# A graph-attention kernel in which TensorE, not VectorE, adds the gathered rows of the second pair of groups

## The chip, the cores and the metric
The kernel runs on one core of a Trainium2 chip. The metric is the device time of one execution in microseconds (us); the median of three runs counts. Engines are named TensorE (PE, its weight loads PEld), VectorE (DVE), ScalarE (ACT), GpSimd (POOL) and SP, which only issues transfers.

## What is computed
Three layers follow one another on 2500 nodes of 256 values: a GATv2 attention over 80000 edges, a lambda layer over all nodes, and a mixture of eight experts. The change touches the attention. Cut to that:

```python
xl = (x @ W_l).reshape(N, HEADS, HEAD_DIM)      # 4 heads of 64
xr = (x @ W_r).reshape(N, HEADS, HEAD_DIM)
e = xl[src] + xr[dst]
e = jnp.where(e >= 0, e, 0.2 * e)
score = jnp.einsum('ehd,hd->eh', e, att)
m = segment_max(score, dst)
ex = jnp.exp(score - m[dst])
agg = segment_sum(ex / segment_sum(ex, dst)[dst] * xl[src], dst)
```

The edges are sorted by destination. The slope is split: 0.8 times the rectified part, made in the loop below, and a linear part that comes in four extra columns of the gathered rows.

## The kernel before
A first stage (`survey`) makes xl and xr and stores them in DRAM; `attend` runs the edges; `node_update` and `experts` follow. The edges are cut into 704 groups of 128, and four groups are a step ("quad"), so there are 176 steps. Eight steps are a run (22 of them), sixteen a turn; the first and last turn are written out, the nine between are a hardware loop. `over_quads` (L928) calls each engine's `quad(q)` in order of steps, and what stands in `quad` is that engine's order of work. Engines meet only by semaphores that count steps.

For step q:
- **GpSimd** (L1069) gathers four times 128 rows of xl, of 260 values, by indirect DMA (L1084) into slot q mod 16 of a ring. It waits for ScalarE's products of step q-14 or so.
- **SP** (L1008) loads the relative destinations and 128 rows of xr (three bf16 parts), once TensorE is through with step q-4.
- **VectorE** makes the selection matrices of step q+2 (`select`, L1150; it waits until TensorE's edge matmuls of step q are done, since it overwrites their buffer), sums, rectifies, scores (L1175), builds the matrices for the sums of step q-10 (`spread`, L1183) and adds step q-12's sums to the running ones (L1197).
- **TensorE** (`edges`, L1394) makes xr[dst] as selection times xr, three bf16 matmuls for each group (L1404). In groups 0 and 1 it also adds xl[src] in PSUM by an fp32 matmul with the identity (L1409). Groups 2 and 3 come first and get no such matmul: VectorE adds their gathered rows (`sum_edges`, L1158) into SBUF. Then come the four matmuls of the sums of step q-12 (L1458).
- **ScalarE** (L1504) makes exponentials and the products with the gathered rows of step q-11 (L1513), sixteen instructions.

The edge sums of a step lie in two PSUM banks, groups 0 and 1 in one, 2 and 3 in the other; steps alternate between two such pairs of banks. The rectified products are L1164 (groups 0 and 1, from PSUM) and L1168 (groups 2 and 3, from the SBUF sum).

When a run is complete, the next eight steps close it: VectorE adds the linear part (L1213) and scans over the scores in step 0, takes the ends (L1230), carries them and makes the drop (L1255) in step 1, raises the tops (L1262, L1268) and takes them off the scores (L1274) in step 2. TensorE turns the scores (L1420, step 1), the ends (L1426, step 1, behind the sums), the carried columns (L1433, step 2) and the tops (L1438, step 3). ScalarE's decay (L1502) waits for the drop, at the front of its step 2, and its products of a new run for L1274.

## Time and profile before
| | us |
|---|---|
| runs | 1641.7, 1633.38, 1640.45; median 1640.45 |
| the profiled execution | 1640.74 |
| its span, first to last instruction | 1639.0 |
| TensorE busy | 1227.7 (75%) |
| VectorE busy | 1081.0 (66%) |
| ScalarE busy | 849.5 (52%) |
| GpSimd busy | 815.9 (50%) |
[...]

Times come from one execution taken by the hardware profiler. "Idle" is the time in which an engine ran nothing ahead of an instruction, and the releaser is what the profile takes for the end of it: "issue" if it shows none, "remote" if the event came from no engine of the list. Matmuls are pipelined, so successive ones overlap in the records, and the step from one start to the next is what they cost in the queue. An fp32 matmul appears as two records.

### The profile page before, as it was taken

The numbers are of one execution on the slowest core, as the hardware profiler recorded it, in microseconds if no ns is written. First come the engines' busy times: TensorE is split into PE (matmuls) and PEld (weight loads), VectorE is DVE, ScalarE is ACT, GpSimd is POOL, SyncE is SP. The second block draws the span as 40 slices with busy tenths as digits, with TensorE's granted clock in tenths as the row PEclk, the third lists the DMA queues.
The fourth block names the chain that finished last, engine by engine and source line by source line (L and its number), as shares of the span: only waits on it lengthen the run. The fifth ranks groups of instructions, "written<-read, shape, count | busy, mean of one in ns | idle before, by whom it ended". The sixth has DMA issues, their size and how long they took to land. (4 is left out here: it accounts for less than half of the span.)

```text
span 1639.0 us, 24939 instructions
## 1 busy us (share of the span) xinstructions
PE 1227.7 (75%) x5659; PEld 873.8 (53%) x5659; DVE 1081.0 (66%) x2307; ACT 849.5 (52%) x3252; POOL 815.9 (50%) x849
## 2 busy tenths in 40 slices
PE   7948677777778777877777876877787656399995
PEld 5426455555555555655555654655565545255663
DVE  8645767676767776777767875777577759304444
ACT  3411466765676566666666755666666713132221
POOL 5344255555565556555565555545656264402223
PEclk9978897888888989898998988888888977599998
DMA  7454356665666656666656665556755125335340
GB/s 183 139 174 121 97 155 162 159 167 149 159 154 166 160 151 159 164 166 163 163 160 165 170 161 152 154 144 169 218 145 138 40 62 174 136 104 148 103 122 17
DMA packets 167497, 237.47 MB, mean 145 GB/s; under 512 B 40112, under 2 KB 134017, under 8 KB 167406
## 3 DMA queue, kind: packets, MB, share of 16 engines
q1 hardware_dynamic: 123310, 130.22, 28.0%
q0 software_dynamic: 41216, 103.67, 24.8%
q10 hardware_dynamic: 2880, 2.66, 0.5%
q14 instruction: 71, 0.58, 0.1%
q8 instruction: 20, 0.33, 0.1%
HBM read 189.57 MB, written 48.91 MB: 146 GB/s over the span
## 5 line engine op out<-in xcount | busy, mean ns | idle before, releaser
L1084 POOL DMA_INDIRECT gathered_rows<-d_xl,e_idx x576 | 547.5, 950 | 430.3 <-ACT e_prod L1513 180.5
L1513 ACT ACTIVATE e_prod<-gathered_rows,e_prod 128x64 f32<-128x64 f32 x2728 | 678.3, 334 | 44.2 <-issue 36.8
L1458 PE MATMUL bank<-e_prod,e_selt 128*128 128x260 f32 x1408 | 407.5, 436 | 141.8 <-DMA gathered_rows<-in_src_dram,n_row_of 73.2
L1458 PEld LDWEIGHTS bank<-e_prod,e_selt 128*128 128x128 f32 x1408 | 289.9, 214 | 235.9 <-DMA gathered_rows<-in_src_dram,n_row_of 86.1
L1404 PE MATMUL bank<-e_xr,e_sel 128*128 128x256 bf16 x2112 | 334.9, 298 | 42.5 <-issue 28.6
L1158 DVE TENSOR_TENSOR e_edge<-bank,gathered_rows 128x512 f32<-128x512 f32 x176 | 119.9, 681 | 292.4 <-remote 269.3
L1404 PEld LDWEIGHTS bank<-e_xr,e_sel 128*128 128x128 bf16 x2112 | 222.3, 107 | 141.1 <-issue 67.7
L1409 PE MATMUL bank<-gathered_rows,ident 128*128 128x256 f32 x704 | 237.6, 418 | 37.8 <-issue 31.2
L1175 DVE TENSOR_REDUCE e_score<-e_edge 128x16 f32<-128x1024 f32 x176 | 213.3, 1212 | 0.3
L1084 POOL DMA_INDIRECT gathered_rows<-d_xl,src_cols x112 | 106.1, 948 | 107.5 <-issue 31.7
L1509 ACT ACTIVATE e_prod<-e_diff 128x16 f32<-128x16 f32 x176 | 39.5, 224 | 207.7 <-remote 136.9
L1409 PEld LDWEIGHTS bank<-gathered_rows,ident 128*128 128x128 f32 x704 | 119.9, 211 | 49.9 <-issue 36.1
L1183 DVE TENSOR_TENSOR e_selt<-bank,cyclic_cols 128x512 f32<-128x512 f32 x176 | 120.0, 682 | 13.8 <-remote 11.2
L1953 POOL DMA_INDIRECT out_dram<-f_out,f_index x32 | 44.8, 1399 | 159.7 <-DVE f_out L2068 154.9
L1164 DVE SCALAR_TENSOR_TENSOR e_edge<-bank,att_relu 128x512 f32<-128x512 f32 x176 | 119.7, 680 | 0.0
L1168 DVE SCALAR_TENSOR_TENSOR e_edge<-e_edge,bank 128x512 f32<-128x512 f32 x176 | 118.8, 675 | 0.0
L1975 PE MATMUL bank<-f_rowst,w_rows 128*128 128x391 f32 x256 | 87.4, 499 | 0.7 <-ACT f_rowst L2016 0.7
L1987 PE MATMUL bank<-f_hid,w_rows 128*128 128x391 f32 x256 | 85.8, 492 | 0.0
L1502 ACT ACTIVATE e_rr<-e_drop 1x4 f32<-1x4 f32 x22 | 4.5, 204 | 156.1 <-DVE e_drop L1255 133.3
L1197 DVE SCALAR_TENSOR_TENSOR e_acc<-e_acc,keep_cols,bank 128x260 f32<-128x260 f32 x154 | 73.6, 478 | 13.4 <-PE bank L1458 10.5
L1975 PEld LDWEIGHTS bank<-f_rowst,w_rows 128*128 128x128 f32 x256 | 49.2, 193 | 37.4 <-issue 2.5
L1987 PEld LDWEIGHTS bank<-f_hid,w_rows 128*128 128x128 f32 x256 | 47.9, 189 | 33.6
(315 smaller groups left out, 1102.2 us busy)
## 6 DMA issues: line engine op xcount, KB each, us to landing
e_xr<-d_xr SPq DMA_DIRECT2D x176, 192.0 KB
d_hist<-e_acc SPq DMA_DIRECT2D x176, 130.0 KB
e_drow<-d_rel SPq DMA_DIRECT2D x176, 128.0 KB
w_rows<-in_L_ffn_w_dram SPq DMA_DIRECT2D x16, 1024.0 KB, 7.2
gathered_rows<-d_xl,e_idx POOLq DMA_INDIRECT x576
d_in<-lambda_w SPq DMA_DIRECT2D x18, 350.7 KB
e_rows<-d_rows SPq DMA_DIRECT2D x22, 192.5 KB
x_rows<-in_x_dram SPq DMA_DIRECT2D x8, 512.0 KB, 4.8
```

Of the source, the lines that this page charges most:

```text
L1084: pool.indirect_dma_start(xl[:, q.slot * G + g, :], None, m.d_xl, bass.IndirectOffsetOnAxis(ap=column, axis=0)).then_inc(gathered[q.slot], 16)
L1158: dve.tensor_tensor(edge[:, b, 2:4, :], ps_edge[b][1][:, :].rearrange("p (g c) -> p g c", g=2), xl[:, q.slot * G + 2:q.slot * G + 4, 0:DIM ...
L1164: dve.scalar_tensor_tensor(out=edge[:, b, 0:2, :], in0=ps_edge[b][0][:, :].rearrange("p (g c) -> p g c", g=2), scalar=0.0, in1=m.att_relu[ ...
L1168: dve.scalar_tensor_tensor(out=edge[:, b, 2:4, :], in0=edge[:, b, 2:4, :], scalar=0.0, in1=att_relu.unsqueeze(1).to_broadcast([P, 2, DIM]) ...
L1175: dve.tensor_reduce(score[:, p, :, q.at * G:q.at * G + G].rearrange("p h g -> p g h"), edge[:, b, :, :].rearrange("p g (h c) -> p g h c", ...
L1183: dve.tensor_tensor(selt[:, b, :, :], lane_up.unsqueeze(1).to_broadcast([P, G, P]), m.cyclic[:, bass.ds(q.k * G, G)].unsqueeze(2).to_broad ...
L1404: last = pe.matmul(out, sel[:, b, g * P:g * P + P], xr[:, r, part * DIM:part * DIM + DIM], start=(part == 0), stop=(part == 2 and g >= 2))
L1409: last = pe.matmul(out, m.ident[:, :], xl[:, q.slot * G + g, 0:DIM], start=False, stop=True)
L1458: last = pe.matmul(ps_agg[b], selt[:, b, g, :], flat(prod[:, b, g, :, :]), start=(g == 0), stop=(g == G - 1))
L1513: last = act.activation(prod[:, b, g, h, 0:HEAD], xl[:, q.slot * G + g, h * HEAD:h * HEAD + HEAD], ACT.Copy, scale=prod[:, b, g, h, HEAD:H ...
L1975: last = pe.matmul(m.bank[2 + f % 2][:, 0:CAP], w1[:, q, half, f * P:f * P + P], rowst[:, q, half, :], start=(half == 0), stop=(half == 1))
L1987: last = pe.matmul(m.bank[4 + to][:, 0:CAP], w2[:, q, f, to * P:to * P + P], hid[:, f, :], start=(f == 0), stop=(f == FCH - 1))
```

## The change
TensorE adds the gathered rows in all four groups, which now go in the order 0, 1, 2, 3. `sum_edges` and its semaphore go. L1168's successor reads the sum from PSUM and the factor from SBUF, so the copy of the factor in PSUM goes too. A new semaphore `half` rises when groups 0 and 1 are done, and the first rectified product waits for it; the second waits for all four. TensorE waits for the second product of step q-2 ahead of group 2.

```diff
-            dve.tensor_copy(att_relu, m.att_relu[:, :]).then_inc(s["fixed"], 1)
...
-            def sum_edges(q):
-                b = q.slot % 2
-                dve.wait_ge(s["edges"], q.k + 1)
-                dve.wait_ge(gathered[q.slot], (q.turn + 1) * 64)
-                if q.since(2):
-                    dve.wait_ge(s["score"], q.k - 1)
-                dve.tensor_tensor(edge[:, b, 2:4, :], ps_edge[b][1][:, :].rearrange("p (g c) -> p g c", g=2),
-                                  xl[:, q.slot * G + 2:q.slot * G + 4, 0:DIM], ALU.add).then_inc(s["summed"], 1)
...
             def relus(q):
 
                 b = q.slot % 2
+                if q.since(2):
+                    dve.wait_ge(s["score"], q.k - 1)
+                dve.wait_ge(s["half"], q.k + 1)
                 dve.scalar_tensor_tensor(out=edge[:, b, 0:2, :], in0=ps_edge[b][0][:, :].rearrange("p (g c) -> p g c", g=2), scalar=0.0,
...
-                dve.wait_ge(s["summed"], q.k + 1)
-                dve.scalar_tensor_tensor(out=edge[:, b, 2:4, :], in0=edge[:, b, 2:4, :], scalar=0.0,
-                                         in1=att_relu.unsqueeze(1).to_broadcast([P, 2, DIM]),
+                dve.wait_ge(s["edges"], q.k + 1)
+                dve.scalar_tensor_tensor(out=edge[:, b, 2:4, :], in0=ps_edge[b][1][:, :].rearrange("p (g c) -> p g c", g=2), scalar=0.0,
+                                         in1=m.att_relu[:, :].unsqueeze(1).to_broadcast([P, 2, DIM]),
...
-                if live:
-                    sum_edges(q)
...
                 if q.since(2):
-                    pe.wait_ge(s["summed"], q.k - 1)
                     pe.wait_ge(s["relu"], 2 * q.k - 3)
-                for g in (2, 3, 0, 1):
+                for g in range(G):
+                    if g == 2 and q.since(2):
+                        pe.wait_ge(s["relu"], 2 * q.k - 2)
                     out = ps_edge[b][g // 2][:, g % 2 * DIM:g % 2 * DIM + DIM]
                     for part in range(3):
                         last = pe.matmul(out, sel[:, b, g * P:g * P + P], xr[:, r, part * DIM:part * DIM + DIM],
-                                         start=(part == 0), stop=(part == 2 and g >= 2))
-                    if g < 2:
-                        if g == 0:
-                            pe.wait_ge(gathered[q.slot], (q.turn + 1) * 64)
-                        last = pe.matmul(out, m.ident[:, :], xl[:, q.slot * G + g, 0:DIM], start=False, stop=True)
+                                         start=(part == 0), stop=False)
+                    if g == 0:
+                        pe.wait_ge(gathered[q.slot], (q.turn + 1) * 64)
+                    last = pe.matmul(out, m.ident[:, :], xl[:, q.slot * G + g, 0:DIM], start=False, stop=True)
+                    if g == 1:
+                        last.then_inc(s["half"], 1)
                 last.then_inc(s["edges"], 1)
...
-                act.wait_ge(s["summed"], q.k - 1)
+                act.wait_ge(s["edges"], q.k - 1)
```

## Rows read from the trace of the kernel before
**Rows 1.** The page's first part: busy time of each engine over the span.
```profile
span 1639.0 us, 24939 instructions
...
PE 1227.7 (75%) x5659; PEld 873.8 (53%) x5659; DVE 1081.0 (66%) x2307; ACT 849.5 (52%) x3252; POOL 815.9 (50%) x849
```

**Rows 2.** Windows, steady loop: us, busy (count) per engine, PEclk, DMA share, GB/s.
```profile
400.00:1100.00 700.00, 523.73 (x2619) 387.05 (x2618) 494.86 (x949) 444.32 (x1830) 397.53 (x419) 0.88 0.60 159
```

**Rows 3.** Groups by line, 400 to 1100 us: count | busy us, mean ns | idle before.
```profile
L1513 ACT ACTIVATE e_prod<-gathered_rows,e_prod 128x64 f32<-128x64 f32 x1674 | 416.4, 335 | 28.2 <-issue 24.3
L1084 POOL DMA_INDIRECT gathered_rows<-d_xl,e_idx x419 | 397.9, 950 | 302.4 <-ACT e_prod L1513 117.6 <-issue 115.4 <-DMA gathered_rows<-in_src_dram,n_row_of 69.4
...
L1409 PE MATMUL bank<-gathered_rows,ident 128*128 128x256 f32 x418 | 139.0, 413 | 22.1 <-issue 22.1
...
L1158 DVE TENSOR_TENSOR e_edge<-bank,gathered_rows 128x512 f32<-128x512 f32 x104 | 70.8, 681 | 170.9 <-remote 159.0 <-PE bank L1409 12.0
L1164 DVE SCALAR_TENSOR_TENSOR e_edge<-bank,att_relu 128x512 f32<-128x512 f32 x104 | 70.7, 680 | 0.0
...
L1168 DVE SCALAR_TENSOR_TENSOR e_edge<-e_edge,bank 128x512 f32<-128x512 f32 x104 | 70.2, 675 | 0.0
```

**Rows 4.** Timeline of VectorE, 700 to 760 us: start us, us, instruction [idle before <-releaser].
```profile
717.57 0.67 DVE L1158 TENSOR_TENSOR e_edge<-bank,gathered_rows 128x512 f32<-128x512 f32 x1
718.17 0.33 DVE L1150 TENSOR_SCALAR e_sel<-e_drow,lane 128x512 bf16<-128x512 bf16 x1
...
726.04 0.69 DVE L1158 TENSOR_TENSOR e_edge<-bank,gathered_rows 128x512 f32<-128x512 f32 x1 [4.22 <-remote]
...
741.12 0.69 DVE L1158 TENSOR_TENSOR e_edge<-bank,gathered_rows 128x512 f32<-128x512 f32 x1 [6.30 <-remote]
```

**Rows 5.** Timeline of TensorE, 700 to 760 us.
```profile
706.59 0.37 PE L1426 MATMUL bank<-ident,e_top 128*1 128x128 f32 x1 [3.20 <-issue]
...
706.97 2.12 PE L1404 MATMUL bank<-e_xr,e_sel 128*128 128x256 bf16 x9
708.89 1.06 PE L1409 MATMUL bank<-gathered_rows,ident 128*128 128x256 f32 x2
709.74 0.62 PE L1404 MATMUL bank<-e_xr,e_sel 128*128 128x256 bf16 x3
...
725.87 0.27 PE L1404 MATMUL bank<-e_xr,e_sel 128*128 128x256 bf16 x1 [1.13 <-issue]
...
726.73 2.02 PE L1458 MATMUL bank<-e_prod,e_selt 128*128 128x260 f32 x8
...
735.74 0.70 PE L1409 MATMUL bank<-gathered_rows,ident 128*128 128x256 f32 x2 [1.92 <-issue]
...
741.04 3.52 PE L1458 MATMUL bank<-e_prod,e_selt 128*128 128x260 f32 x8 [2.96 <-DMA gathered_rows<-in_src_dram,n_row_of]
...
748.34 1.15 PE L1404 MATMUL bank<-e_xr,e_sel 128*128 128x256 bf16 x9
749.32 0.60 PE L1409 MATMUL bank<-gathered_rows,ident 128*128 128x256 f32 x2
749.75 0.49 PE L1404 MATMUL bank<-e_xr,e_sel 128*128 128x256 bf16 x3
...
753.18 2.72 PE L1458 MATMUL bank<-e_prod,e_selt 128*128 128x260 f32 x8 [2.40 <-DMA gathered_rows<-in_src_dram,n_row_of]
758.52 0.37 PE L1426 MATMUL bank<-ident,e_top 128*1 128x128 f32 x1 [2.62 <-issue]
```

**Rows 6.** Timeline of GpSimd, 700 to 760 us.
```profile
714.53 0.94 POOL L1084 DMA_INDIRECT gathered_rows<-d_xl,e_idx  x1 [5.08 <-ACT e_prod L1513]
...
741.78 0.94 POOL L1084 DMA_INDIRECT gathered_rows<-d_xl,e_idx  x1 [2.93 <-DMA gathered_rows<-in_src_dram,n_row_of]
```

**Rows 7.** Timeline of ScalarE, 700 to 760 us.
```profile
711.36 0.20 ACT L1502 ACTIVATE e_rr<-e_drop 1x4 f32<-1x4 f32 x1 [5.57 <-DVE e_drop L1255]
```

**Rows 8.** Windows of 2 us around one standstill, columns as in rows 2.
```profile
738.00:740.00 2.00, 0.08 (x1) 0.00 (x0) 0.00 (x0) 0.00 (x0) 0.85 (x1) 0.50 0.47 114
```

More of the change, by code:

```diff
@@ L942, in attend @@
     sb = lambda name, shape, dt=F32: ctx.enter_context(nc.sbuf_tensor(name, shape, dt))
-    s = sem_set(nc, m.sems, "att", "init idx sel edges summed relu score lin turned run top ends heads fwd bwd carried drop cols raised tops topped diff rr f fac ex prod selt agg old acc rows* links fixed shares")
+    s = sem_set(nc, m.sems, "att", "init idx sel half edges relu score lin turned run top ends heads fwd bwd carried drop cols raised tops topped diff rr f fac ex prod selt agg old acc rows* links fixed shares")
     sl = sem_set(nc, m.sems, "lam", "chain less e ctxps ctx wqps wq turnedps turned lamps lam var rstd bn mixps mix rowed x clear")
@@ L993, in attend @@
     ps_fac = m.bank[6][:, 3 * P + 4:3 * P + 4 + HEADS]
-    att_relu = m.bank[7][:, 0:DIM]
     lane_up = m.bank[7][:, DIM:DIM + P]
@@ L1107, in _ @@
             dve.wait_ge(s["init"], 4)
-            dve.wait_ge(s["fixed"], 2)
+            dve.wait_ge(s["fixed"], 1)
             lamed = Chain(dve, sl["chain"], 0)
```

2 lines of the change are left out of this document (1 added, 1 removed).

## The prediction

> **What bounds the kernel now.** The page's first part [rows 1] is read first: no engine is full over the span of 1639.0 us. TensorE has 75% of it, VectorE 66%, ScalarE 52%, GpSimd 50%. A share this low says that waits, not one engine, set the time, so the steady loop has to be read by itself. The window from 400 to 1100 us [rows 2] holds some 104 steps, so a step takes 6.7 us: TensorE is busy 523.73 us of 700, VectorE 494.86, at a mean granted clock of 0.88. The groups by line of that window [rows 3] say what a step holds and where the idle time lies. VectorE's whole idle time but a little stands ahead of one instruction, the sum at L1158 (170.9 us); TensorE's ident matmuls (L1409) have 22.1 us ahead of them; GpSimd's gathers have 302.4 us, of which only 117.6 by ScalarE's products.
>
> The three timelines show the rhythm. A run of eight steps takes 51.93 us (L1426 starts at 706.59 and at 758.52 [rows 5]). In it VectorE works without a gap up to 721.8 us, then stands for 4.22 us, and for 6.30 us before 741.12 [rows 4]. These gaps aren't VectorE's own: TensorE stops inside a matmul group and goes on at 725.87 (1.13 us), at 741.04 (2.96) and at 753.18 (2.40) [rows 5], GpSimd at 741.78 (2.93) [rows 6], and between 738 and 740 us nearly everything stands but a gather's issue [rows 8]. I call these the standstills. The profile doesn't name what ends them; they come while GpSimd issues gathers back to back, and their last releasers are called "remote" or a gather DMA. What the reader is to see: outside the standstills VectorE and TensorE are **both** nearly full, and the change moves work from one to the other.
>
> **The change, part by part.**
> - *The sum on VectorE goes.* L1158 lasts 681 ns [rows 3], but the next instruction starts 0.60 us after it (717.57 to 718.17 [rows 4]), so its queue gets 0.60 us a step shorter: 176 steps, 106 us in all, 4.8 us in a run. VectorE's work in a run was 494.86/700 x 51.93 = 36.7 us and becomes 31.9.
> - *The second product reads PSUM and its factor from SBUF.* That is the form of L1164 (680 ns) instead of L1168's (675) [rows 3]: under 1 us in the whole kernel; I take nothing, covered by the 0.60 above.
> - *TensorE gets two more fp32 ident matmuls a step.* At the full clock the next instruction starts 0.43 us after such a pair of records (749.32 to 749.75); at clock 0.5 it was 0.85 (708.89 to 709.74) [rows 5]. Two a step are 0.86 us at the high clock, 1.7 at the low one; 352 of them are 151 to 299 us. In a run: 16 x 0.43 = 6.9 us, or 6.9/0.88 = 7.8 at the loop's mean clock [rows 2].
> - *What of that is exposed.* TensorE's busy time in a run is 523.73/700 x 51.93 = 38.9 us. With 7.8 more it is 46.7, and with the three standstills (1.1 + 3.0 + 2.4 = 6.5 us [rows 5]), in which it can't work, 53.2, or 1.3 more than the run of 51.93. With the additions all at the full clock it is 52.3, or 0.4 more. So the slack is just used up: the wait for the scan ahead of L1426 (3.20 and 2.62 us) and the one for late rows (1.92 at 735.74) are the cover. If that cover were not usable, because those waits stay where they are, 3.2 + 1.9 = 5.1 us a run would come on top. I take 0.8 a run, the middle of 0.4 and 1.3, since the scan comes earlier when VectorE's queue shortens and its wait is the nearest thing to be filled. Over the 21 runs that have this rhythm: 17 us.
> - *The gather's wait moves.* Today nine selection matmuls (748.34 to 749.32, 0.98 us [rows 5]) run before TensorE waits for the gathered rows; then only three do, and 6/9 x 0.98 = 0.65 us of work lies behind the wait that lay before it. In 400 to 1100 us 22.1 us of waits stand at L1409 [rows 3], about 1.6 in a run, so this costs at most 2 x 0.65 = 1.3 us a run where TensorE is the bound. Behind the wait in TensorE's queue are the whole step's sums (L1458), the closing transposes, and so ScalarE and the add of sums. I put it inside the range, not in the sum. VectorE loses its own gather wait; nothing, since TensorE had met the same one already.
> - *"Half".* The first product waits for half of a step's matmuls. But in VectorE's queue the selection for step q+2 (L1150) stands ahead of it, and that waits for all edge matmuls of step q (the buffer's last reader). So the new semaphore is never the last wait, except in the last two steps, which select nothing. I count nothing; were it to work, it could hide up to 2 x (0.33 + 0.43) = 1.5 us of a step where VectorE waits for TensorE (0.33 is 749.75 to the next ident matmul, a third of the nine's 0.98).
> - *Waits on buffers.* At its first group TensorE waits for the first product of step q-2, as before; the second product is now waited for at the third group. That product ends 0.6 us after the first, and the third group comes 2 x (0.33 + 0.43) = 1.5 us after the first one's start, so the wait is never later than the old one: nothing.
> - *The next sources on ScalarE* wait for the matmuls of an earlier step instead of its sum: earlier, nothing. SP's loads wait for those same matmuls, three steps ahead: 0.86 us later of some 20, nothing. The copy of the factor to PSUM at the start goes: 0.3 us at most, once.
>
> The sum: -4.8 us a run on VectorE, which hides; +0.8 on TensorE, which shows. The profiled execution took 1640.7 us for its span of 1639.0, and it lies at the median of the runs (1640.45). 1641 + 17 = **1658 us**.
>
> *A rule that speaks the other way.* The low clock in this case follows TensorE's stops: 0.50 in 738 to 740 us, and the next group of sums takes 3.52 us [rows 5, 8]; the nine selection matmuls after the 3.20 us wait take 2.12 us against 1.15 later [rows 5]. [...] By that rule more ident matmuls in the gaps would bring time back instead of costing it; what that would give here is a rival below.
>
> **The rivals.**
> - *A, the forecast: TensorE becomes the bound.* Speaks for it: 38.9 + 7.8 + 6.5 us against 51.93. Against: VectorE has no gap either in most stretches. If the waits don't fill, +1.9 us a run, 1681; with 1.3 for the moved gather wait and part of the 3.2, up to +2.8, 1700. Own range 1649 to 1700.
> - *B, nothing moves: gathers set the pace.* GpSimd issues 32 gathers in a run, one each 1.25 us (950 ns and 0.30 us of issue), 40 us, and each burst ends in a standstill. If the standstills belong to the gathers, any engine that stays below the run's 51.93 us is hidden: 1641. For it: ahead of 741.78 GpSimd waits for a DMA by the profile, not for an engine [rows 6]. Against: the 117.6 us that ScalarE's products cost it.
> - *C, faster: the closing chain shortens.* GpSimd waits 5.08 us at 714.53 for products of ScalarE [rows 6], and ScalarE has waited 5.57 us for the drop that VectorE makes at the end of step 1 [rows 7]. VectorE has two sums fewer before that (steps 0 and 1), 1.2 us a run, and has no gap there. If this chain sets the run, 21 x 1.2 = 25 us go: 1616. It decides as long as TensorE has its scores turned and its edges ready by then, that is, as long as TensorE's 1.7 us more in these two steps fit into the 2.6 to 3.2 us that it now waits at L1426. Against: the same run's next step needs TensorE's transposes, and those come 0.86 us a step later.
> - *D, faster: the clock comes back.* [...] Low-clock losses in a run: 3.52 - 2.02 (a group of sums at 726.73) = 1.5, 2.72 - 2.02 = 0.7, 2.12 - 1.15 = 1.0 and 1.06 - 0.60 = 0.5 [rows 5], 3.7 us. The standstills stay, and with them what follows 741.04, so about two thirds come back, 2.4 us a run, or 50 us: 1658 - 50 = 1608. For it: the mean clock of 0.88 [rows 2] leaves room. Against: TensorE's stops are not made by its own lack of work.
> - *E, the change doesn't do what it says:* the "half" part has no effect, which is already in A to D.
>
> **How the numbers follow.** A 0.46, B 0.24, C 0.18, D 0.12. The most likely is A, 1658. Limits of what can be told are 0.5%, 8 us, around 1641. Faster: C and D, 0.30. Same: B, 0.24. Slower: A, 0.46. The range takes A to its bound less its last few us, all of B, all of C and down to D's number: 1608 to 1695. The far ends, -106 us (all of VectorE's saving) and +151 (all matmuls exposed), are left out, since neither engine is alone in the critical stretches.
>
> **What would show it.** Right: TensorE's busy time in 400 to 1100 us near 87 to 90%, VectorE's near 61%; the wait ahead of L1426 shorter than 3 us; VectorE's idle time now ahead of the selection, with which its step begins, and released by the ident matmuls instead of "remote"; a run of 52.5 to 53 us. Wrong, to C or D: a run below 51, GpSimd's 5.08 us shorter, a granted clock above 0.92. Wrong, to B: GpSimd's waits and the run's length unchanged. If the standstills themselves grow or vanish, I have mistaken their cause, and the forecast with it.

## The result, and the profile after

The change makes the kernel slower. After: 1697.61 us, the median of four runs (1685.64 to 1703.01), beside 1641.08 us for the kernel before in the same comparison. The ratio is 1.033, with a 95% interval of 1.027 to 1.040. The forecast was 1658 us, in a range of 1608 to 1695: the direction was right, the size was not (17 us forecast, 57 measured), and the result lies outside the range. The profiled execution took 1697.8 us for a span of 1696.1.

The page's first part of the kernel after, to be read against [rows 1]:

```profile
span 1696.1 us, 25994 instructions
...
PE 1349.5 (80%) x6363; PEld 971.2 (57%) x6363; DVE 979.5 (58%) x2130; ACT 849.0 (50%) x3252; POOL 817.6 (48%) x849
```

TensorE's share rises from 75 to 80%, VectorE's falls from 66 to 58%. TensorE has 704 more matmul records and as many more weight loads. The same 700 us of the steady loop as in [rows 2], with the same columns:

```profile
400.00:1100.00 700.00, 573.43 (x2909) 426.79 (x2909) 419.95 (x819) 423.44 (x1747) 379.91 (x400) 0.91 0.58 152
```

TensorE is busy 573.43 us and not 523.73, VectorE 419.95 and not 494.86. The mean granted clock, a share of the full one, rose from 0.88 to 0.91. Two starts of the turned ends in TensorE's timeline give the length of two runs:

```profile
516.10 0.27 PE L1418 MATMUL bank<-ident,e_top 128*1 128x128 f32 x1 [1.89 <-DVE e_top L1217]
...
625.57 0.37 PE L1418 MATMUL bank<-ident,e_top 128*1 128x128 f32 x1 [2.62 <-DVE e_top L1217]
```

That is 109.47 us, 54.7 for each; before it was 51.93 [rows 5], which is one of the shortest of its window. Over all starts of these instructions in the window, twelve runs each, a run took 53.2 us before (440.5 to 1078.4 us) and 56.2 us after (400.5 to 1074.3). So a run grew by 3.0 us. TensorE's work in it went from 523.73/700 x 53.2 = 39.8 us to 573.43/700 x 56.2 = 46.0, 6.2 more, and its idle time from 13.4 us to 10.2, 3.2 less. About half of the added work was hidden in idle time. The groups by line say what idle time is left, 400 to 1100 us (count | busy, mean ns | idle before). Three of TensorE's groups before, beside L1409 in [rows 3]:

```profile
L1458 PE MATMUL bank<-e_prod,e_selt 128*128 128x260 f32 x837 | 243.9, 439 | 94.3 <-DMA gathered_rows<-in_src_dram,n_row_of 54.9 <-issue 26.8 <-ACT e_prod L1513 12.2
L1404 PE MATMUL bank<-e_xr,e_sel 128*128 128x256 bf16 x1260 | 197.2, 296 | 10.9 <-issue 8.9 <-DVE e_edge L1164 0.8 <-DVE e_edge L1168 0.8
...
L1426 PE MATMUL bank<-ident,e_top 128*1 128x128 f32 x13 | 4.3, 329 | 44.2 <-DVE e_top L1225 23.4 <-issue 20.8
```

And those of the kernel after:

```profile
L1083 POOL DMA_INDIRECT gathered_rows<-d_xl,e_idx x400 | 380.3, 951 | 322.4 <-ACT e_prod L1505 188.1 <-issue 112.6 <-DMA gathered_rows<-in_src_dram,n_row_of 21.7
L1399 PE MATMUL bank<-gathered_rows,ident 128*128 128x256 f32 x802 | 268.7, 416 | 40.8 <-issue 28.5 <-DMA gathered_rows<-d_xl,e_idx 12.1
L1395 PE MATMUL bank<-e_xr,e_sel 128*128 128x256 bf16 x1204 | 218.5, 289 | 36.5 <-issue 36.2
L1450 PE MATMUL bank<-e_prod,e_selt 128*128 128x260 f32 x800 | 210.5, 405 | 20.2 <-issue 17.6 <-ACT e_prod L1505 2.4
...
L1156 DVE SCALAR_TENSOR_TENSOR e_edge<-bank,att_relu 128x512 f32<-128x512 f32 x100 | 68.0, 680 | 0.0
L1160 DVE SCALAR_TENSOR_TENSOR e_edge<-bank,att_relu 128x512 f32<-128x512 f32 x100 | 67.8, 678 | 0.0
...
L1148 DVE TENSOR_SCALAR e_sel<-e_drow,lane 128x512 bf16<-128x512 bf16 x100 | 35.4, 354 | 168.8 <-remote 122.9 <-PE bank L1399 45.2 <-issue 0.6
...
L1418 PE MATMUL bank<-ident,e_top 128*1 128x128 f32 x13 | 4.1, 316 | 31.8 <-DVE e_top L1217 25.5 <-issue 6.3
```

In the kernel after L1399 is the identity matmul, L1395 the selection, L1450 the sums, L1156 and L1160 the rectified products, L1148 VectorE's selection, L1418 the turned ends. VectorE still waits 168.8 us, now ahead of the selection with which its step begins, and 122.9 of it still end at "remote".

TensorE has 28.5 + 36.2 + 17.6 = 82.3 us of idle time marked "issue" ahead of its three main groups. Before, the same label has 22.1 + 8.9 + 26.8 = 57.8 us. That isn't the whole of it: the other 54.9 us are put down to a gather of `in_src_dram`, and all six of those gathers were issued between 17.8 and 25.3 us. They can't end a wait after 400 us, and one of these waits is the 2.96 us ahead of 741.04 that the prediction counts as a standstill [rows 5]. Both labels together are 112.7 us before and 82.3 after, or 8.6 and 6.6 us a run. TensorE's wait ahead of the turned ends, where it needs VectorE's scan, is 44.2 us before and 31.8 after, or 3.4 and 2.6 a run. The waits for gathered rows are 12.1 us, 1.0 a run. GpSimd waits more for ScalarE's products, 188.1 us where it was 117.6 [rows 3]. Its 69.4 us before and 21.7 after under the name of the same gather are as little a wait for it.

What a standstill looks like from inside shows in TensorE's timeline of the kernel after:

```profile
703.46 0.27 PE L1395 MATMUL bank<-e_xr,e_sel 128*128 128x256 bf16 x1 [0.76 <-issue]
705.57 0.27 PE L1395 MATMUL bank<-e_xr,e_sel 128*128 128x256 bf16 x1 [1.84 <-issue]
706.97 0.37 PE L1395 MATMUL bank<-e_xr,e_sel 128*128 128x256 bf16 x1 [1.13 <-issue]
707.69 1.22 PE L1399 MATMUL bank<-gathered_rows,ident 128*128 128x256 f32 x2 [0.34 <-issue]
...
714.35 0.49 PE L1395 MATMUL bank<-e_xr,e_sel 128*128 128x256 bf16 x3
714.68 0.60 PE L1399 MATMUL bank<-gathered_rows,ident 128*128 128x256 f32 x2
715.11 0.49 PE L1395 MATMUL bank<-e_xr,e_sel 128*128 128x256 bf16 x3
```

Three selection matmuls of one group, with no wait between them in the program, start at 703.46, 705.57 and 706.97 us. At 714.35 three of them take 0.33 us together, and a group with its identity matmul 0.76 (714.35 to 715.11). The steps from start to start in the first stretch are 2.11, 1.40 and 0.72 us. TensorE isn't stopped for good there: it starts one matmul after each of these steps, and no row shows what holds the next one back. SP, the engine that only issues transfers, goes through the same stops: in the kernel before, the timeline has no start on any engine after 737.90 until SP's at 741.02, TensorE at 741.04, VectorE at 741.12 and ScalarE at 741.28.

The runs that follow need one remark. The same kernel before took 1640 to 1655 us in some groups of runs and 1405 us in others, on several chips, two of which (called 7 and 15 in the results) showed both; so every ratio is given against the runs of before in its own group. The two are told apart by the trace: I laid the timelines of TensorE, VectorE and ScalarE over each other, and of 700 us (400 to 1100) all three are idle at once for 99 us in the kernel before as first profiled, for 73 in the kernel after, and for 1 to 8 us in the traces of the groups at 1405 us. The fall from 99 to 73 isn't the change's: the same two kernels in a later group show 102 and 108 us. I call them "with standstills" and "without" below. The change was measured with them.

### The profile page after: what moved, and what is told of

Its sections match the earlier page's. It is cut to its first block and busy times, and to the rows that moved or that the text cites. A ratio compares the mean times of both kernels' runs of the same rounds, so it can differ in the third digit from the quotient of the medians.

```text
span 1696.1 us, 25994 instructions
## 1 busy us (share of the span) xinstructions
PE 1349.5 (80%) x6363; PEld 971.2 (57%) x6363; DVE 979.5 (58%) x2130; ACT 849.0 (50%) x3252; POOL 817.6 (48%) x849
## 5 line engine op out<-in xcount | busy, mean ns | idle before, releaser
L1399 PE MATMUL bank<-gathered_rows,ident 128*128 128x256 f32 x1408 | 471.0, 416 | 62.7 <-issue 43.7
L1395 PE MATMUL bank<-e_xr,e_sel 128*128 128x256 bf16 x2112 | 385.2, 290 | 66.5 <-issue 57.5
L1450 PE MATMUL bank<-e_prod,e_selt 128*128 128x260 f32 x1408 | 367.5, 404 | 37.1 <-issue 22.8
L1450 PEld LDWEIGHTS bank<-e_prod,e_selt 128*128 128x128 f32 x1408 | 276.3, 201 | 103.3 <-issue 53.0
L1395 PEld LDWEIGHTS bank<-e_xr,e_sel 128*128 128x128 bf16 x2112 | 216.5, 104 | 207.4 <-issue 106.1
L1399 PEld LDWEIGHTS bank<-gathered_rows,ident 128*128 128x128 f32 x1408 | 237.0, 209 | 88.8 <-issue 54.9
L1148 DVE TENSOR_SCALAR e_sel<-e_drow,lane 128x512 bf16<-128x512 bf16 x176 | 63.5, 361 | 321.0 <-remote 239.8
L1501 ACT ACTIVATE e_prod<-e_diff 128x16 f32<-128x16 f32 x176 | 39.8, 226 | 290.8 <-remote 208.3
L1083 POOL DMA_INDIRECT gathered_rows<-d_xl,src_cols x112 | 106.4, 950 | 110.7 <-ACT e_prod L1505 33.4
L1156 DVE SCALAR_TENSOR_TENSOR e_edge<-bank,att_relu 128x512 f32<-128x512 f32 x176 | 119.8, 681 | 0.0
L1160 DVE SCALAR_TENSOR_TENSOR e_edge<-bank,att_relu 128x512 f32<-128x512 f32 x176 | 119.4, 678 | 0.0
```

Source lines behind the costliest of these rows:

```text
L1083: pool.indirect_dma_start(xl[:, q.slot * G + g, :], None, m.d_xl, bass.IndirectOffsetOnAxis(ap=column, axis=0)).then_inc(gathered[q.slot], 16)
L1156: dve.scalar_tensor_tensor(out=edge[:, b, 0:2, :], in0=ps_edge[b][0][:, :].rearrange("p (g c) -> p g c", g=2), scalar=0.0, in1=m.att_relu[ ...
L1160: dve.scalar_tensor_tensor(out=edge[:, b, 2:4, :], in0=ps_edge[b][1][:, :].rearrange("p (g c) -> p g c", g=2), scalar=0.0, in1=m.att_relu[ ...
L1395: last = pe.matmul(out, sel[:, b, g * P:g * P + P], xr[:, r, part * DIM:part * DIM + DIM], start=(part == 0), stop=False)
L1399: last = pe.matmul(out, m.ident[:, :], xl[:, q.slot * G + g, 0:DIM], start=False, stop=True)
L1450: last = pe.matmul(ps_agg[b], selt[:, b, g, :], flat(prod[:, b, g, :, :]), start=(g == 0), stop=(g == G - 1))
```

## The experiments

**First group, without standstills** (before at 1405.5 us). `p1_pe_only` gives the kernel before two more fp32 identity matmuls a step, of rows that lie still, and keeps VectorE's sum:

```diff
                 for g in (2, 3, 0, 1):
                     out = ps_edge[b][g // 2][:, g % 2 * DIM:g % 2 * DIM + DIM]
+                    if g >= 2:
+                        pe.matmul(out, m.ident[:, :], m.xnt[:, g, :], start=True, stop=False)
...
-                                         start=(part == 0), stop=(part == 2 and g >= 2))
+                                         start=(part == 0 and g < 2), stop=(part == 2 and g >= 2))
```

> The kernel before, with two more fp32 identity matmuls a step on TensorE (rows that lie still in SBUF, so no new wait), VectorE's sum kept. It computes something else: groups 2 and 3 get a constant tile added. Theory (TensorE's added work is not hidden by its own gaps): slower than the kernel after, or like it, 1695 to 1730 us, since VectorE's 0.6 us a step is not given back. Rival (the time goes with the moved gather wait or the order of groups, not with the work): within 10 us of before, 1641. Second rival (TensorE's clock comes back with more work): 1641 or below, clock above 0.89.

Measured: 1388.1 us, 0.991 of before (0.986 to 0.996). Faster by 0.9%, the second rival's sign; the times that were expected were for the other kind of run, here and in the next three. Its window of 400 to 1000 us:

```profile
400.00:1000.00 600.00, 579.51 (x3305) 465.31 (x3303) 546.41 (x1046) 473.08 (x1980) 433.95 (x456) 0.99 0.77 205
```

TensorE is busy 579.51 of 600 us at a clock of 0.99. Without standstills it is full, and the kernel isn't slower for it.

`p2_dve_only` is the kernel after without the two added matmuls:

```diff
-                    last = pe.matmul(out, m.ident[:, :], xl[:, q.slot * G + g, 0:DIM], start=False, stop=True)
+                    if g < 2:
+                        last = pe.matmul(out, m.ident[:, :], xl[:, q.slot * G + g, 0:DIM], start=False, stop=True)
```

> The kernel after without the two added identity matmuls: the gathered rows of groups 2 and 3 are left out of the sums. VectorE has its sum off, TensorE has the work of before, with the gather wait at its new place. Theory (VectorE and TensorE were both nearly full, and VectorE's queue is worth something): faster than before, 1600 to 1625. Rival (gathers set the pace whatever VectorE does): 1635 to 1650.

Measured: 1414.83 us, 1.010 (1.007 to 1.014). VectorE's relief, with the order and the wait of the change, brings nothing here; the theory's gain isn't there.

`p3_half_first` splits `relus` in two and puts the first rectified product, now `first_relus`, ahead of the selection in VectorE's step (the split is left out of the cut):

```diff
+                if live:
+                    first_relus(q)
                 if at == 2:
                     raise_tops(o)
                 if not q.known() or q.k + 2 < QUADS:
                     select(q.ago(-2))
```

> The kernel after with the first rectified product ahead of the selection in VectorE's queue, so that it really begins when groups 0 and 1 are done. Theory (the wait for half is masked by the selection's wait for the whole step, and VectorE now waits for TensorE in a part of the steps): 10 to 30 us faster than after, 1670 to 1688. Rival (VectorE has slack everywhere now, so its latency is worth nothing): 1693 to 1702.

Measured: 1423.17 us, 1.017 (1.010 to 1.025). Against the kernel after without standstills (1.016, in the third group) it is no gain. The wait for half is masked in the change by the reading of the code, and L1156 has 0.0 us of idle time ahead of it, but unmasking it is worth nothing that shows.

`p4_order` is the kernel before with groups in the order 0, 1, 2, 3:

```diff
-                for g in (2, 3, 0, 1):
+                for g in range(G):
```

> The kernel before with groups in the order 0, 1, 2, 3, so that TensorE meets the wait for gathered rows after three selection matmuls in place of nine; the sum stays on VectorE. Theory (the moved wait costs up to 1.3 us a run where rows are late): 1645 to 1665. Rival (no cost): 1636 to 1646.

Measured: 1416.14 us, 1.004 (0.997 to 1.011): no difference that can be told. The wait itself is there. The groups of 400 to 1000 us, first of this kernel:

```profile
L1409 PE MATMUL bank<-gathered_rows,ident 128*128 128x256 f32 x428 | 144.0, 420 | 101.0 <-DMA gathered_rows<-d_xl,e_idx 99.9 <-DMA gathered_rows<-d_xl,src_cols 1.0
```

and of `p1_pe_only`, where nine selection and two constant matmuls stand ahead of the wait:

```profile
L1411 PE MATMUL bank<-gathered_rows,ident 128*128 128x256 f32 x454 | 141.0, 393 | 20.5 <-DMA gathered_rows<-d_xl,e_idx 20.1 <-DMA gathered_rows<-d_xl,src_cols 0.2
```

101.0 us of waits for gathered rows against 20.5, at times 2% apart. Much of that is TensorE being less busy, 484.00 us of 600 in `p4_order` against 579.51: `e12_sp_events` below, which has the order and the matmuls of before, waits 81.2 us at the same place. So the order adds at most some 20 us to these waits and nothing that shows to the time.

**Second group, with standstills** (before at 1653 us). `e5_after_again` and `e6_before_again` are the two kernels unchanged.

> The kernel after, unchanged, on the chip on which the first four experiments ran (the kernel before takes 1405 us there, and their traces show no standstill of all engines). Theory (after the fall of the first one: added TensorE work brings its clock back, and what costs is the wait for gathered rows that now stands ahead of more work): 1415 to 1435, 1.01 to 1.02 of before, waits for gathered rows at the identity matmuls above 40 us in 600. Rival (the loss of 3.3% is TensorE's bound itself): 1450 or more, TensorE busy above 97% of the steady loop.

Measured: 1704.83 us, 1.029 (1.021 to 1.036), where 1.01 to 1.02 was expected for the other condition. The wait for the scan is 56.1 us in 700 here, for 12 runs:

```profile
L1418 PE MATMUL bank<-ident,e_top 128*1 128x128 f32 x12 | 4.0, 330 | 56.1 <-DVE e_top L1217 52.4 <-issue 3.7
```

> The kernel before, unchanged, for its trace on this chip. Theory: no stop of all engines at once, waits for gathered rows at L1409 between 20 and 60 us in 600, clock 0.92. Rival (the standstills are there and merely shorter): idle time released by remote ahead of L1158 above 50 us in 600.

Measured: 1645.45 us, 0.997 (0.992 to 1.002), the same kernel against itself, which is a measure of what the comparison can tell. The rival came true: 163.6 us of "remote" ahead of L1158. The profiled execution took 1659.67 us. Its groups are the second measure of TensorE's idle time before:

```profile
L1458 PE MATMUL bank<-e_prod,e_selt 128*128 128x260 f32 x809 | 240.4, 443 | 77.4 <-DMA gathered_rows<-in_src_dram,n_row_of 33.4 <-issue 29.3 <-ACT e_prod L1513 13.2
L1404 PE MATMUL bank<-e_xr,e_sel 128*128 128x256 bf16 x1224 | 194.2, 300 | 12.4 <-issue 9.6 <-DVE e_edge L1168 1.6 <-DVE e_edge L1164 1.1
...
L1409 PE MATMUL bank<-gathered_rows,ident 128*128 128x256 f32 x408 | 138.4, 418 | 28.5 <-issue 26.2 <-DMA gathered_rows<-d_xl,e_idx 2.2
...
L1426 PE MATMUL bank<-ident,e_top 128*1 128x128 f32 x13 | 4.4, 341 | 60.4 <-DVE e_top L1225 49.1 <-issue 11.3
```

"Issue" and the gather of `in_src_dram` are 29.3 + 9.6 + 26.2 + 33.4 = 98.5 us. The wait for the scan is 60.4 us, 4.6 a run, and 4.7 in `e5_after_again`: in this pair of executions nothing of it was filled.

`e7_late_gather_wait` takes the selections of groups 0 and 2, then the wait, an identity matmul for each, and then the selections of 1 and 3 with theirs:

```diff
-                for g in range(G):
+                for g in (0, 2, 1, 3):
...
+                    if g == 2:
+                        pe.wait_ge(gathered[q.slot], (q.turn + 1) * 64)
+                    if g in (2, 3):
+                        for h in (g - 2, g):
+                            last = pe.matmul(target(h), m.ident[:, :], xl[:, q.slot * G + h, 0:DIM], start=False, stop=True)
```

> The kernel after with its matmuls in another order: selections of groups 0 and 2, then the wait for gathered rows, which now has six selection matmuls ahead of it in place of three; then the selections of 1 and 3, each followed by two identity matmuls. Theory (the gather wait's place costs): 5 to 15 us faster than after. Rival (its place costs nothing, the sum of the work does): within 5 us of after. The first product begins later, which VectorE's queue masks by its selection.

Measured: 1702.97 us, 1.028 (1.022 to 1.035), within 2 us of the kernel after. The rival: the place of the wait costs nothing here.

`e8_after_lead16` changes one number:

```diff
-LEAD = 14
+LEAD = 16
```

> The kernel after with gathers that wait only for the last reader of their own ring slot, step q-16, in place of step q-14 (LEAD 16), so that rows arrive about two steps earlier. Theory (late rows ahead of the identity matmuls make the loss): waits for gathered rows at the identity matmuls fall below 10 us in 600, and the kernel is at or under before, 1380 to 1410. Rival (TensorE's own work is the bound): the waits go, but the time stays within 8 us of after.

Measured: 1704.8 us, 1.028 (1.022 to 1.035). Earlier gathers change nothing. With standstills there was little to win: in `e5_after_again` TensorE waits for gathered rows only 4.0 us in 700.

**Third group, without standstills** (before at 1404.4 us).

> The kernel after, unchanged, as the yardstick of this group of runs. Where all engines have standstills (before at 1640 to 1655 us): 1.027 to 1.035 of before. Where there are none (before at 1405 us): 1.012 to 1.022.

Measured: 1424.5 us, 1.016 (1.009 to 1.023). The waits of 400 to 1000 us (us in all, times, longest):

```profile
DVE e_sel L1148 <- PE bank L1399: 61.5, 54, 5.4
...
PE bank L1399 <- DMA gathered_rows<-d_xl,e_idx: 43.9, 26, 2.8
```

> The same kernel as p1_pe_only (two identity matmuls a step more on TensorE with no new wait, sum kept on VectorE). It ran at 0.991 of before where there are no standstills. Theory (standstills grow with what the engines issue, and TensorE's added matmuls are issued whatever they wait for): 1.02 to 1.04 of before where there are standstills, nearly all of the change's loss. Rival (the loss is in the new dependence on gathered rows, not in the work): 0.985 to 1.005.

Measured: 1378.77 us, 0.982 (0.975 to 0.990): as in the first group, faster. Theory and rival were for runs with standstills; this says nothing of either, nor does the next.

> The same kernel as p2_dve_only (VectorE's sum off, no matmul in its place, gather wait at its new place). It ran at 1.010 of before where there are no standstills. Theory (standstills follow the issued work): 0.98 to 1.00 where there are standstills. Rival (the order of groups and the wait cost): 1.01 to 1.02.

Measured: 1412.96 us, 1.007 (1.003 to 1.011). Parts and whole don't add up without standstills: -1 to -2% and +0.7 to 1.0% against +1.6% together.

`e12_sp_events` adds instructions on an engine that has time:

```diff
                 sp.dma_start(m.d_hist[bass.ds(q.k * P, P), :], flat(acc[:, r, :, :])).then_inc(stored[r], 16)
+                for _ in range(16):
+                    settle(sp, m)
```

> The kernel before with 16 more semaphore increments a step on SP, behind its store; nothing waits for them, each takes 17 ns. They are 2816 instructions more, against 1055 more in the change's profile. Theory (the standstills grow with the number of instructions that any engine issues): 40 us or more slower, where there are standstills, and nothing where there are none. Rival (the standstills have to do with TensorE's work or with transfers, not with a count of instructions): within 8 us of before.

Measured: 1392.4 us, 0.993 (0.989 to 0.996). It was to tell something about standstills and met none, so it doesn't. An increment takes 17 ns in its trace (the median on SP), so a step gets 16 x 17 ns = 0.27 us more on SP. It is a sign that delays of 0.3 us there can move this kernel by 0.7%; the kernel before against itself came out 0.3% off.

**Fourth group, with standstills** (before at 1648.6 us). The two parts again, in the condition of the measured change.

> The same kernel as p1_pe_only, in the hope of the state of the machine in which the change was measured (before at 1640 to 1655 us, standstills in the trace). Theory (TensorE's added matmuls lengthen the run there, since standstills cut into a TensorE that has less slack): 1.015 to 1.035 of before. Rival (the loss hangs on the gathered rows): 0.98 to 1.00, as where there are no standstills. Where before is at 1405 it repeats 0.982 to 0.991.

Measured: 1715.97 us, 1.034 (1.024 to 1.044). The sign is turned against the groups without standstills, and the size is that of the whole change. Its window:

```profile
400.00:1100.00 700.00, 563.41 (x2874) 429.12 (x2875) 475.55 (x913) 419.30 (x1723) 370.12 (x391) 0.91 0.57 149
```

Busy 563.41 of 700: not full by a wide margin, yet slower.

> The same kernel as p2_dve_only (VectorE's sum gone, no matmul added, the gather wait at its new place). With standstills: theory 0.98 to 1.00, rival (the wait's place and the order cost) 1.01 to 1.02. Without them it repeats 1.007 to 1.010.

Measured: 1655.59 us, 1.0035 (1.001 to 1.006). VectorE's sum off, with the order and the gather wait of the change, is worth nothing and costs next to nothing.

`f3_sums_first` puts TensorE's sums of step q-12 ahead of its edge matmuls:

```diff
+                first = q.since(CLOSE_LAG) and q.at != 4
+                if first:
+                    sums(q.ago(CLOSE_LAG))
                 if q.exists():
                     edges(q)
...
-                if q.since(CLOSE_LAG):
+                if q.since(CLOSE_LAG) and not first:
                     sums(q.ago(CLOSE_LAG))
```

> The kernel after with TensorE's sums of step q-12 ahead of the edge matmuls of step q, except in the fourth step of a run, so that nothing old is queued behind the wait for gathered rows. Theory (what is queued behind the wait, the sums and with them ScalarE's products and the next gathers, carries the loss): 10 to 30 us faster than after, that is 0.99 to 1.01 of before without standstills (after is at 1.016), 1.01 to 1.02 with them (after is at 1.029 to 1.033). Rival (the edge sums themselves come too late for VectorE): like after or slower, since they come 1.8 us later.

Measured: 1854.13 us, 1.123 (1.118 to 1.129), far past the rival. The waits of its 400 to 1100 us:

```profile
POOL gathered_rows L1083 <- ACT e_prod L1508: 271.5, 75, 13.5
DVE e_sel L1148 <- remote: 171.9, 19, 14.6
...
DVE e_diff L1266 <- PE bank L1430: 56.9, 11, 6.6
...
PE bank L1450 <- ACT e_prod L1508: 38.7, 23, 3.0
```

Every engine now waits in turn: TensorE for products of ScalarE, with the new edges behind that wait, VectorE for the tops that TensorE turns and, longest, ahead of its selection, GpSimd 271.5 us for products. By these waits the edge matmuls had been the work that hid ScalarE's products; that isn't tested by itself.

**Fifth group, one kernel, with standstills** (before at 1645.9 us). `f4_wide_ident` adds the gathered rows of each pair of groups in one matmul of 512 columns, ahead of their selections:

```diff
+                for h in range(2):
...
+                    pe.matmul(ps_edge[b][h][:, :].rearrange("p (g c) -> p g c", g=2), m.ident[:, :],
+                              xl[:, q.slot * G + 2 * h:q.slot * G + 2 * h + 2, 0:DIM], start=True, stop=False)
+                    for g in (2 * h, 2 * h + 1):
...
+                            last = pe.matmul(out, sel[:, b, g * P:g * P + P], xr[:, r, part * DIM:part * DIM + DIM],
+                                             start=False, stop=(part == 2 and g % 2 == 1))
```

> The kernel after with one fp32 identity matmul of 512 columns for each pair of groups in place of two of 256, and first in its pair: the same columns and so the same time on TensorE, half the identity matmuls and weight loads (8 records of TensorE fewer in a step, as many as in the kernel before), and the wait for gathered rows at the very front. Theory (what costs is TensorE's time): within 8 us of after, 1.012 to 1.02 of before without standstills, 1.025 to 1.035 with them. Rival (what costs where there are standstills is the number of instructions that TensorE issues): 1.00 to 1.015 there. Second rival (with rows late, a wait ahead of everything adds): 1.02 or more without standstills.

Measured: 1676.89 us, 1.017 (1.009 to 1.024), half of the loss. That is clear of the 1.027 to 1.040 of the change's own comparison, but it touches the 1.021 to 1.036 of `e5_after_again`, and the kernel after didn't run in this group. TensorE's timeline shows that a pair takes the time that it took:

```profile
709.23 1.02 PE L1395 MATMUL bank<-gathered_rows,ident 128*128 128x512 f32 x2
710.09 0.82 PE L1400 MATMUL bank<-e_xr,e_sel 128*128 128x256 bf16 x6
710.74 1.02 PE L1395 MATMUL bank<-gathered_rows,ident 128*128 128x512 f32 x2
```

From 709.23 to 710.74 are 1.51 us for a pair; the change takes 0.76 us a group (714.35 to 715.11 above), 1.52 for two. The groups:

```profile
L1395 PE MATMUL bank<-gathered_rows,ident 128*128 128x512 f32 x398 | 228.3, 658 | 16.5 <-issue 14.2 <-DMA gathered_rows<-d_xl,e_idx 1.6 <-DVE e_edge L1156 0.4
L1452 PE MATMUL bank<-e_prod,e_selt 128*128 128x260 f32 x800 | 217.8, 419 | 50.9 <-DMA gathered_rows<-in_src_dram,n_row_of 31.6 <-issue 13.7 <-ACT e_prod L1507 5.5
L1400 PE MATMUL bank<-e_xr,e_sel 128*128 128x256 bf16 x1189 | 175.1, 283 | 14.2 <-issue 14.1
```

14.2 + 14.1 + 13.7 = 42.0 us are marked "issue", where the kernel after had 82.3; with the 31.6 us put down to the gather of `in_src_dram` it is 73.6. So most of that difference is one of labels, and 8.7 us of 700 are left. The expectation's "within 8 us of after" fell, and its rival, 1.00 to 1.015, missed by little: the loss seems to be neither all time nor all count.

**Sixth group, with standstills** (before at 1643.7 us). `f5_before_wide` makes the two identity matmuls of the kernel before one:

```diff
                     if g == 0:
                         pe.wait_ge(gathered[q.slot], (q.turn + 1) * 64)
+                        pe.matmul(ps_edge[b][0][:, :].rearrange("p (g c) -> p g c", g=2), m.ident[:, :],
+                                  xl[:, q.slot * G:q.slot * G + 2, 0:DIM], start=True, stop=False)
...
-                    if g < 2:
-                        if g == 0:
-                            pe.wait_ge(gathered[q.slot], (q.turn + 1) * 64)
-                        last = pe.matmul(out, m.ident[:, :], xl[:, q.slot * G + g, 0:DIM], start=False, stop=True)
```

> The kernel before with its two identity matmuls a step (groups 0 and 1) made one of 512 columns, first in its pair: the same time on TensorE, 4 records of TensorE fewer in a step (704 in all), VectorE's sum kept. The wait for gathered rows now has six selection matmuls ahead of it in place of nine. Theory (with standstills a part of the time goes with the number of instructions that TensorE issues): 0.985 to 0.997 of before where there are standstills, 0.995 to 1.01 where there are none. Rival (the count is nothing; f4 gained by its order): 0.998 to 1.01 in both.

Measured: 1639.36 us, 0.996 (0.990 to 1.002). The middle is where the theory had it, but the interval holds 1. It is the fastest kernel with standstills that computes the reference, and it isn't shown to beat the one before.

```profile
L1458 PE MATMUL bank<-e_prod,e_selt 128*128 128x260 f32 x848 | 240.8, 432 | 106.4 <-DMA gathered_rows<-in_src_dram,n_row_of 52.0 <-ACT e_prod L1513 36.5 <-issue 17.8
L1408 PE MATMUL bank<-e_xr,e_sel 128*128 128x256 bf16 x1260 | 193.1, 293 | 9.2 <-issue 7.4 <-DVE e_edge L1164 1.6
...
L1405 PE MATMUL bank<-gathered_rows,ident 128*128 128x512 f32 x210 | 122.8, 670 | 18.0 <-issue 13.0 <-DMA gathered_rows<-d_xl,e_idx 4.9
```

Its "issue" sum is 13.0 + 7.4 + 17.8 = 38.2 us, against 57.8 in the kernel before and 65.1 in `e6_before_again`. With the gather of `in_src_dram` it is 90.2 against 112.7 and 98.5.

`f6_tiny_matmuls` adds four matmuls of two columns a step:

```diff
+                for _ in range(4):
+                    pe.matmul(ps_edge[b][0][:, 0:2], sel[:, b, 0:P], xr[:, r, 0:2], start=True, stop=True)
                 for g in (2, 3, 0, 1):
```

> The kernel before with four more bf16 matmuls of two columns a step on TensorE, in a region that the step overwrites afterwards: 8 records of TensorE more a step, as many as the change adds, with little time of their own (a weight load of 0.11 us each at most, 0.43 us a step against the change's 0.86). Theory (count and time both cost where there are standstills): 1.01 to 1.02 there, 0.995 to 1.005 where there are none. Rival (time alone): 1.00 to 1.01 in both. Second rival (count alone): 1.025 or more there.

Measured: 1693.33 us, 1.025 (1.017 to 1.032), above the theory's 1.01 to 1.02 and at the lower edge of the second rival, count alone. The timeline of its weight loads says what the four take outside a standstill:

```profile
706.23 0.37 PEld L1402 LDWEIGHTS bank<-e_xr,e_sel 128*128 128x128 bf16 x4
706.53 0.88 PEld L1406 LDWEIGHTS bank<-e_xr,e_sel 128*128 128x128 bf16 x9
```

0.30 us from the first to what follows. Its groups and a slow stretch of TensorE in its timeline:

```profile
L1460 PE MATMUL bank<-e_prod,e_selt 128*128 128x260 f32 x800 | 227.9, 428 | 27.0 <-issue 21.4 <-ACT e_prod L1515 4.9
L1406 PE MATMUL bank<-e_xr,e_sel 128*128 128x256 bf16 x1205 | 201.8, 296 | 86.5 <-issue 86.2
...
L1411 PE MATMUL bank<-gathered_rows,ident 128*128 128x256 f32 x400 | 141.0, 434 | 13.4 <-issue 12.4 <-DMA gathered_rows<-d_xl,e_idx 0.7
...
L1402 PE MATMUL bank<-e_xr,e_sel 128*128 128x2 bf16 x400 | 25.3, 166 | 4.2 <-issue 4.0
```

```profile
703.02 1.13 PE L1460 MATMUL bank<-e_prod,e_selt 128*128 128x260 f32 x4
704.46 0.38 PE L1460 MATMUL bank<-e_prod,e_selt 128*128 128x260 f32 x1 [0.31 <-issue]
705.19 0.38 PE L1460 MATMUL bank<-e_prod,e_selt 128*128 128x260 f32 x1 [0.35 <-issue]
705.91 0.70 PE L1460 MATMUL bank<-e_prod,e_selt 128*128 128x260 f32 x2 [0.34 <-issue]
```

The "issue" sum is 86.2 + 12.4 + 21.4 + 4.0 = 124.0 us, and nothing is put down to the gather of `in_src_dram`; before, the two labels have 112.7 and 98.5. It is the only kernel of those with standstills that has more of this idle time than both traces of before. In the slow stretch three records of the sum matmuls start 0.73 and 0.72 us apart (704.46, 705.19, 705.91), each with a gap marked "issue", while VectorE works (L1168 at 704.51, L1285 at 705.10); outside it, eight of them take 2.02 us (the group at 726.73 of before [rows 5]), 0.25 each.

## Why the prediction was wrong, point by point

- *TensorE becomes the bound (rival A, the forecast)*: right in the engine, shown by `f1_pe_only` (1.034) beside `f2_dve_only` (1.0035). TensorE's added matmuls alone give the change's whole loss where there are standstills.
- **The step that failed is the exposed part: 0.8 us a run.** It measured 3.0 by the mean run of the window, 2.7 by the whole time (57 us over 21 runs). The prediction's sum for a run was 38.9 us of work, 7.8 added and 6.5 of standstills, 53.2, with nothing for the waits. Measured: 46.0 us of work in all, where it had 46.7; 6.6 us of idle time marked "issue", where it had 6.5; and 2.6 us of waits for the scan and 1.0 for gathered rows, where it had none. So what failed is that the slack would be filled: 3.6 us a run of it stayed open. The prediction had this case, as "if that cover were not usable", and let it count only in rival A's own range, up to 1700, not in the 0.8. In the later pair of executions the scan's wait didn't shrink at all, 4.6 us a run before and 4.7 after. Part of the cover was never there: the 1.92 us at 735.74, taken for late rows, are marked "issue", as are all 22.1 us ahead of L1409 [rows 3], and in the last 0.71 of them all three engines stand. And 51.93 us was a short run; a mean one had 8.6 us of standstills in TensorE and not 6.5, so that 6.5 agrees with what stayed is luck: some 2 us a run of standstills, in which TensorE "can't work" by the prediction, were filled (1.0 in the later pair, 98.5 and 79.7 us in 700).
- *Why the added work hides so little* is shown in part. I had priced the added matmuls by their time and not by their number. `f6_tiny_matmuls` speaks for the number: 0.30 us a step at the change's number cost 1.025. `f4_wide_ident` speaks for both: the same time at the old number cost 1.017. An estimate by subtraction: 1.7% for the 0.86 us (`f4_wide_ident`) leaves 1.2 to 1.6% of the change's 2.9 to 3.3% for eight more records a step, matmuls and weight loads, and 2.5% less a third of 1.7 leaves 1.9% (`f6_tiny_matmuls`). The intervals are 0.7% to either side, so the split is rough. Two rivals aren't separated from it. The clock moved with the number: 0.905 to 0.915 over the span in `f4_wide_ident` where the kernel after had 0.889 to 0.897, and 0.855 to 0.864 in `f6_tiny_matmuls` where before had 0.863 to 0.878. And `f4_wide_ident` also moved the gather wait, which `e7_late_gather_wait` (1.028 where the kernel after has 1.029) and `p4_order` (1.004, 0.997 to 1.011) found to cost nothing that can be told.
- *VectorE's 4.8 us a run hide*: right. Its relief, with the new order and wait, brought nothing in either condition: 1.010 and 1.007 without standstills, 1.0035 with them.
- *"Half" has no effect*: the code masks it, as said; the 1.5 us that unmasking might bring didn't come without standstills (1.017 against 1.016); with them it wasn't tried.
- *The moved gather wait, up to 1.3 us a run*: TensorE waits for rows 12.1 us in 700 in the kernel after, 1.0 a run, and 4.0 us in `e5_after_again`. That is a part of the idle time above, but moving the wait (`e7_late_gather_wait`, 1702.97 us) or the gathers (`e8_after_lead16`, 1704.8) won nothing against the 1704.83 of `e5_after_again`.
- *SP, the next sources, the second product's operands*: L1160, the successor of L1168, takes 678 ns in the kernel after where L1168 took 675 [rows 3], as said; no trace pointed at the other two.
- *Rival B, gathers set the pace*: wrong. The run grew with the same number of gathers, and earlier gathers changed nothing (`e8_after_lead16`, 1704.8 us against 1704.83). The sign that it rested on, the wait ahead of 741.78 [rows 6], was put down to a gather of the first 26 us and was none.
- *Rival C, the closing chain shortens*: wrong here. GpSimd's waits for ScalarE's products grew from 117.6 to 188.1 us.
- *Rival D, the clock comes back*: it does in part, from 0.88 to 0.91 in the window, and it doesn't pay with standstills (1.033). That a denser TensorE gets more of the clock was an assumption in its 50 us: the four tiny matmuls a step of `f6_tiny_matmuls` left 0.855 to 0.864 over the span, where before had 0.863 to 0.878. Without standstills the two added matmuls alone (`p1_pe_only`, `e10_pe_only`) gave 0.991 and 0.982 at a clock of 0.945 against 0.92. That the clock is the cause of that gain isn't shown; `e12_sp_events` has 0.993 with no matmul added.
- *What would prove me wrong*: "if the standstills themselves grow or vanish, I have mistaken their cause". They vanished in the groups at 1405 us (1 to 8 us of 700), for both kernels, so the gathers, which the prediction named beside them, don't make them by themselves. That the change itself alters them isn't shown: the time in which three engines stand at once was 99 and 102 us before, 73 and 108 after.
- *The signs*: TensorE's busy time was to be 87 to 90% of the window and is 82%, which is the unfilled slack again. VectorE's 60% is as said, near 61. The wait ahead of the turned ends is 2.4 us on each of the 13 instructions, under 3 as said, but 4.7 in `e5_after_again`. VectorE's idle time went to the selection as said, though it is mostly still "remote" (122.9 us) and not the identity matmuls' (45.2).

Open: what a standstill is. That it isn't in either kernel is shown by the 1405 us of the same program. The queue that the page calls "instruction" (q14) doesn't tell the two conditions apart: it moved 0.58 MB in 71 packets in the kernel before as in `p4_order`, and in 400 to 1100 us one took 0.35 us on average in the one and 0.37 in the other. The recording itself is a rival that no run here can test, since every execution on record has a span and a clock and so was recorded. Other work on the chip at the same time is another. Whether instructions of other engines count as TensorE's do wasn't met by `e12_sp_events`. Why the parts don't add up without standstills (0.99 and 1.01, together 1.016) wasn't tried further.

## What to carry to other kernels

Before work is moved to an engine that has idle time, see what each wait is for. A wait for another engine's result can stay open when work is added: TensorE's for the scan was 4.6 us a run before and 4.7 after in the later pair. Count the added instructions as well as their time: with standstills four tiny matmuls a step, 0.30 us, cost 2.5% here, and the change's added time at the old number of matmuls cost 1.017 in place of 1.029 to 1.033. A releaser is to be believed only if it ran near the wait that it is said to end: here gathers of the first 26 us were named for waits after 400. One execution's shortest run is no yardstick (51.93 us, where the window's mean was 53.2); take the mean of a window, and two executions. This program ran at 1405 and at 1650 us without a change in it, and two more identity matmuls a step came out at 0.991 in the one condition and 1.034 in the other, so a part of a change must be measured against the kernel before in the same group of runs. Price a relieved engine at nothing until something is found that waited for it: 0.60 us a step off VectorE gave 1.0035 to 1.010 of before, no gain.

## What was not expected of the hardware

- The same program took 1405 us and 1650 us in different groups of runs, on two chip numbers each in both; what the traces show of the difference is stops that all engines share.
- TensorE can slow to one matmul record each 0.72 us inside a group that has no wait, while VectorE works on (704.46 to 705.91 in `f6_tiny_matmuls`); in the kernel after steps of 2.11, 1.40 and 0.72 us follow one another, close to three, two and one times 0.7.
- Four tiny matmuls a step, 0.30 us outside a standstill and 53 us in all 176 steps, cost 1693.33 - 1643.71 = 50 us. Two identity matmuls a step, 0.86 us or 151 us in all, cost 1715.97 - 1648.64 = 67 us. Both add 704 matmul records.
- Sums put ahead of edge matmuls, the same instructions in another order, took 1854.13 us (`f3_sums_first`), 1.123 of before, where the kernel after has 1.029 and 1.033.
